# Forty unit-matrix products on TensorE around the start of attention, into a PSUM bank that nobody reads

## The reference

```python
x = x + quantised_product(layernorm(x), ctx)                 # L0_xattn
x = x + moe(layernorm(x), 32 experts, top 4, 1 shared)       # L0_ffn
q, k, v = layernorm(x), ctx, ctx                             # L1_xattn, h = 8 heads
qk = jnp.einsum('bhdq,bhdl->bhql', qh, kh) * scale
sm = jax.nn.softmax(qk, axis=-1)
ret = jnp.einsum('bhql,bhdl->bhdq', sm, vh)
x = x + gamma * ret
x = x + moe(layernorm(x), 8 experts, top 2, 2 shared)        # L1_ffn
```

## Time and profile before

| what | us |
|---|---|
| median of 3 executions | 422.51 |
| lowest and highest of them | 420.99, 424.89 |
| the profiled execution, its own time | 424.28 |
| its span, first to last instruction | 422.5 |
| PE busy in the span | 346.8 (82%) |
| DVE busy | 262.6 (62%) |
| ACT busy | 194.7 (46%) |
| POOL busy | 183.0 (43%) |

### The profile page before, as it was taken

One profiled execution on the slowest core, in us unless ns is written; L12 is line 12 of the kernel. 1 busy time (PEld: TensorE's weight loads), 2 busy tenths in 40 slices (PEclk: granted clock), 3 DMA queues, 4 the chain that ended last, 5 costly groups with the idle time before them and its releaser, 6 DMA issues.

```text
span 422.5 us, 8097 instructions
## 1 busy us (share of the span) xinstructions
PE 346.8 (82%) x2303; PEld 191.8 (45%) x2303; DVE 262.6 (62%) x722; ACT 194.7 (46%) x453; POOL 183.0 (43%) x338
## 2 busy tenths in 40 slices
PE   0003298789999999999999738999986799998997
PEld 0002194444554554554554425565564344544454
DVE  2999848625555555555555496699977455555174
ACT  1341254344555555555553146799932455553110
POOL 2000301266766766766753127446620656763100
PEclk9999999999999999999999965799985999999899
DMA  7999991049223223224464579600002222331531
GB/s 235 387 267 318 341 263 58 1 137 282 88 88 97 88 92 98 90 90 95 134 180 132 199 278 281 193 1 2 2 2 100 69 82 89 102 87 51 167 108 50
DMA packets 28297, 57.31 MB, mean 136 GB/s; under 512 B 3807, under 2 KB 12735, under 8 KB 28255
## 3 DMA queue, kind: packets, MB, share of 16 engines
q1 hardware_dynamic: 20110, 37.85, 29.0%
q0 software_dynamic: 6528, 17.83, 13.9%
q10 hardware_dynamic: 1616, 1.11, 0.9%
HBM read 44.72 MB, written 12.06 MB: 134 GB/s over the span
## 4 chain that ended last, share of the span: by engine, by line
PE 69%; DVE 15%; issue 6%; POOL 4%; ACT 3%; DMA 2%; DVEq 0%; SPq 0%; ACTq 0%; POOLq 0%
PE bank L1308 22%; PE bank L1337 14%; PE bank L1319 6%; PE bank L1187 6%; PE bank L1299 4%; PE bank L1386 3%; PE bank L1398 3%; PE bank L1226 2%; PE bank L1200 2%; DMA x_sb<-x 2%; DVE st L733 1%; DVE x_sb L1025 1%; PE bank L1154 1%; PE bank L1181 1%; PE bank L1305 1%
## 5 line engine op out<-in xcount | busy, mean ns | idle before, releaser
L1308 PE MATMUL bank<-arena,xT 128*64 x272 | 111.2, 491 | 1.1 <-ACT xT L631 1.1
L1311 PE MATMUL bank<-xn,xT 128*64 128x384 f32 (+1 forms) x272 | 111.2, 491 | 0.0
L516 POOL DMA_INDIRECT xg<-m_xn,tab x68 | 66.2, 974 | 60.4 <-PE bank L1299 30.6
L505 POOL DMA_INDIRECT m_ys<-ysb,dest x68 | 67.2, 988 | 38.9 <-DVE ysb L945 22.5
L1337 PE MATMUL bank<-arena,hT 96*64 (+1 forms) x272 | 70.6, 381 | 2.2 <-DVE hT L931 2.1
L1340 PE MATMUL bank<-xn,hT 96*64 96x256 f32 (+1 forms) x272 | 70.7, 382 | 0.0
L624 ACT ACTIVATE xn<-arena 128x768 f32 (+1 forms) x68 | 56.3, 827 | 22.5 <-issue 22.5
L957 DVE TENSOR_TENSOR hh<-sg,bank 128x192 f32<-128x192 f32 (+1 forms) x71 | 24.8, 349 | 60.1 <-ACT sg L647 60.1
L1337 PEld LDWEIGHTS bank<-arena,hT 96*64 96x64 f32 (+1 forms) x272 | 34.8, 135 | 39.5 <-issue 29.2
L631 ACT ACTIVATE xT<-bank 128x256 f32<-128x256 f32 x71 | 27.2, 384 | 47.8 <-PE bank L1299 47.0
L925 DVE COPY xn<-arena 96x512 f32 (+1 forms) x68 | 29.3, 430 | 23.5 <-issue 23.5
(11 more groups left out here) (180 smaller groups left out, 562.5 us busy)
## 6 DMA issues: line engine op xcount, KB each, us to landing
arena<-w_gu SPq DMA_DIRECT2D x3, 3456.0 KB, 21.2
arena<-w_dn SPq DMA_DIRECT2D x3, 1728.0 KB, 26.5
arena<-m_ys SPq DMA_DIRECT2D x8, 512.0 KB, 5.7
arena<-w_gu SPq DMA_DIRECT2D x2, 1408.0 KB
m_xn<-xn SPq DMA_DIRECT2D x2, 1024.0 KB, 7.6
arena<-m_ys SPq DMA_DIRECT2D x8, 256.0 KB, 3.4
arena<-w_dn SPq DMA_DIRECT2D x2, 704.0 KB
arena<-w_gu SPq DMA_DIRECT2D x1, 1152.0 KB
```

What stands on the lines that cost most here:

```text
L505: nc.gpsimd.indirect_dma_start(out=ys_d[L.name], out_offset=bass.IndirectOffsetOnAxis(ap=dest[:, s:s + 1], axis=0), in_=ysb[:, s % BUFS, : ...
L516: nc.gpsimd.indirect_dma_start(out=xg[:, b, :], out_offset=None, in_=xn_d[L.name], in_offset=bass.IndirectOffsetOnAxis(ap=d["tab"][:, s:s ...
L1308: T.matmul(bank[2 + s % 2][0:BLOCK, 0:2 * J2], xT[:, s % 2, c, 0:BLOCK], arena[:, bass.ds(off + c * 2 * J2, 2 * J2)], start=(c == 0), stop ...
L1311: return T.matmul(bank[2 + s % 2][BLOCK:P, 0:2 * J2], xT[:, s % 2, c, BLOCK:P], gu2[:, s % 2, cols], start=(c == 0), stop=(c == C - 1), ti ...
```

## The change

A helper unread(n) issues n products of the 128x128 unit matrix with itself, float32, 128 columns each, into the first 128 columns of bank 5. They wait for no semaphore and raise none, and nothing reads what they write. Twenty-six of them stand ahead of scores(0), and fourteen behind turn_p(0), ahead of scores(2).

```diff
                                  start=(k == 0), stop=(k == 1), tile_position=(0, h * HEAD))
                 ins.then_inc(av_done, 1)
 
+            def unread(n):
+
+                for _ in range(n):
+                    T.matmul(bank[5][:, 0:P], ident[:], ident[:], start=True, stop=True)
+
+            unread(26)
             scores(0)
             scores(1)
             for p in range(nheads // 2):
                 turn_p(2 * p)
+                if p == 0:
+                    unread(14)
                 if p + 2 < nheads // 2:
                     scores(p + 2)
```

## The result

The changed kernel takes 417.94 us (median of 6, 416.78 to 419.93) where the kernel before takes 422.56 (6 runs). The ratio is 0.9873, with a 95% interval of 0.9845 to 0.9901. The forecast was 419.0 in a range of 416.6 to 422.0, with a chance of 0.55 on a change within 1% and of 0.41 on a kernel that is more than 1% faster; the measured one is 1.3% faster.

What follows compares the result with a forecast made beforehand. TensorE at the low clock was taken to bound the kernel between 255.4 and 269 us. 424.28 less 5.8 plus 1.0 gave 419.5, from the median 417.7; 419.0 was taken, range 416.6 to 422.0.

Steps and rivals of the forecast that it cites:

- Where the loss lay: Attention from scores(2) at 255.38 us: the low clock costs nothing earlier; the full clock gains 5.8 us after it.
- First block: 26 products ahead of scores(0): 0.217 us each, 5.6 us in all, hidden in the wait with 0.7 us to spare.
- Second block at full clock: 14 products between turn_p(0) and scores(2): 3.0 us, ending at 254.7, hidden with 0.7 us to spare.
- The fall in the hole, plus 1.0 us: Idle gap ahead of turn_p(0): the clock falls in most executions, the second block takes 4.6 us, scores(2) 1.0 us late.
- From 424.28 to the median: Whole kernel: profiled sum 419.5, from the median 417.7; 419.0 taken, as other runs may have a shorter low stretch.
- The second fall: Attention after 255.4: the clock falls again at about 258.7, back at 269; about 420.7 us, chance 0.18.
- The block as the new wait: Second block starts low, clock not lifted before 269: scores(2) 3.0 us late, 427.3 or 425.5 us; chance 0.07.
- The slower end: Whole kernel: over 426.7 us, the dearest part of the rivals that predict a loss; chance 0.04.
- unit matrices would not count: Both blocks: nearly all-zero products might not move the clock; a loss up to 427, or 422.5 us; chance 0.07.

Runs made afterwards that it cites:

- e1: The changed kernel with the second block of 14 products taken out, only the 26 ahead of scores(0) kept: 423.89 us, ratio 1.0011 to the kernel before.
- e6: The changed kernel measured once more with nothing altered: 419.57 us, ratio 0.9917 to the kernel before.
- e3: The changed kernel with each product of both blocks replaced by two transposes of the unit matrix: 417.91 us, ratio 0.9864 to the kernel before.
- e7: The changed kernel with its second block doubled from 14 to 28 products: 421.97 us, ratio 0.9961 to the kernel before.
- e4: The changed kernel with products of 8 columns instead of 128 in both blocks: 430.0 us, ratio 1.0171 to the kernel before.
- e5: The changed kernel with a third block of 8 products between scores(1) and turn_p(0): 418.86 us, ratio 0.9891 to the kernel before.

## Why the prediction was right

**Where the loss lay.** Right. The low clock cost nothing until scores(2), and 5.9 us behind it: from scores(2) to scores(15) it was 45.62 us before and is 39.74 after. The step had 5.8. Its parts hold as well: from scores(2) to scores(3) it gained 1.8 us (the step had 1.7), from scores(3) to scores(5) 4.1 (4.4 less 0.3), and the 0.3 us of waiting for tile 2 are there, 0.28 us ahead of scores(4) at 259.32. Small slip: the 3.97 us of the working takes its two ends from two views; the timeline alone gives 3.90.

**First block.** Right: 0.112 us a record and 5.97 us in all where I had 0.109 and 5.6, hidden. What the prediction doesn't say is that it gains nothing alone (e1).

**Second block at full clock.** 3.29 us against 3.0, hidden.

**The fall in the hole, plus 1.0 us.** The mechanism is there, its size was off. The price is not one number: 1.9 us in e6, where the clock was low for 4.9 us of the block, and 0.6 in e3, where it was low for 2.1; the working had 3.1 us low and a price of 1.0. How often the fall comes is less well known: I put it "in most executions", and one of three profiles of the changed kernel has it, but so have three of the five that run the same code up to the end of turn_p(0). At 1.9 us each, that makes 0.6 to 1.1 us on average. So the 1.0 of the sum is not refuted as an average, but it fits by luck: no profile of the changed kernel shows it, they show 0 or 1.9.

**From 424.28 to the median.** This is the weak step. The sum takes off 4.8 us. The medians fell by 4.6, 3.5 and 5.3 us in the three measurements (0.9873, 0.9917, 0.9880), so the sum from the median, 417.7, was the better one, and going up to 419.0 took off only 3.5. My reason for it, that the other runs have a shorter low stretch, is not shown. What is shown is another source: the first score scatters over 3.5 us in eleven profiles, from code ahead of the change. By this step a change within 1% became the likelier outcome in the forecast (0.55 against 0.41), and it isn't what was measured here; of the three ratios one is within 1%.

**Rivals.** The second fall did not come: no profile of the changed kernel has one between 257 and 300, and the Trainium skill's rule that would have made it likely ("TensorE: Matmul & The Clock Gate", Part 4) is contradicted by e3. The block as the new wait exists, and e7 prices it at one for one. The slower end is real for a filler of 8-column products (e4: 1.7% slower). That unit matrices would not count is out, with both products and transposes.

## What to carry to other kernels

Look for the stage where a low clock and a busy TensorE coincide, and put dense filler, products back to back, right ahead of it, in waits that another engine's chain holds open anyway; e1 shows that filling the longest wait is worth nothing if the clock then falls in the next hole. Not every filler does it: products of 8 columns kept PE busy by the profile, and the clock fell (e4). And it must end before the operand that PE waits for arrives, for each microsecond too much is a microsecond at the end. Price it at both clocks, since the block that repairs a fall begins at the lower one.

## What was not expected of the hardware

The clock column of a profile can't be read before its first change. In e5 four records of a 384-column product took 2.77 us at 74.86, and three took 1.13 us at 80.14, though the windows show 1.00 for both:

```profile
74.86 2.77 PE L1154 MATMUL bank<-arena 128*128 128x384 f32 x4
...
80.14 1.13 PE L1154 MATMUL bank<-arena 128*128 128x384 f32 x3
```

```profile
75.00:77.00 2.00, 2.00 (x5) 1.09 (x4) 2.00 (x2) 0.38 (x1) 0.00 (x0) 1.00 0.00 0
...
80.00:81.00 1.00, 1.00 (x5) 0.71 (x5) 1.00 (x2) 0.38 (x1) 0.00 (x0) 1.00 0.00 0
```

Less the last record's own 0.85 and 0.49 us, that is 0.64 us from record to record, and 0.32 later: the two levels, 1.2 and 2.4 GHz. The first four records of this line, at about 62.5, take 2.79 to 2.91 us in all twelve profiles, where four take 1.46 at the full clock. So the first MoE stage begins at the low clock in every profile, and where the low clock ends differs between executions of the same code. That is a candidate for the scatter of the first score; no run here tried it.
